# Small array tiles side by side in TensorE's order, a first join in four column groups, and a tap moved to ScalarE and GpSimd

## The chip, the cores and the metric

The kernel runs on one core of one Trainium2 chip. The metric is the device time of one launch in microseconds (us).

## The reference

The input is x, of shape (8, 1024, 128) in float32. A layer of gated linear attention with 8 heads of 128 comes first, then a mixture of 8 experts of which each token takes 2. The change touches the attention alone:

```python
q = _short_conv(x @ Wq, conv_q)                     # 8 heads; conv of 4 taps along time, then SiLU
k, v = _short_conv(x @ Wk, conv_k), _short_conv(x @ Wv, conv_v)   # 8 heads x 3 Householder steps each
beta, g = 2 * sigmoid(x @ Wb), -exp(A_log) * softplus(x @ Wa + dt_bias)
q, k = _l2norm(q) * d ** -0.5, _l2norm(k)
for t in time:                                      # S: one 128x128 state per head
    S = S * exp(g_t)
    for i in range(3):
        S = S + beta_i * outer(k_i, v_i - k_i @ S)
    o_t = q_t @ S
out = (rmsnorm(o) * silu(x @ Wg)) @ Wo              # then residual and layer norm
```

`_short_conv` adds four products: the input shifted by 0, 1, 2 and 3 tokens, each times a weight of its channel (a tap each), and takes SiLU of the sum.

## The kernel before

The 8192 tokens go through 64 superchunks of 128 tokens, of which each has four chunks (c = 0 to 3) of 32 tokens. A chunk has 32 x 3 = 96 rows of k and v, one for each Householder step. The recurrence over a chunk is written as a triangular system of 96x96 for each head, whose inverse is built in three diagonal blocks of 32 and joined from them.

Work is software-pipelined. In step (i, c) the engines project superchunk i (function `project`), prepare the chunk four before (gram products, `U`, `UQ`, `KD`), invert the diagonal blocks of the chunk five before, and run the chunk six before (join, solve, new state, read-out). Each step has 14 slots, k = 0 to 13, and in each slot one of the superchunk's 56 projection tiles (24 of v, 24 of k, 8 of q) is made. Four engines each follow a program of their own, in order, and meet at semaphores. The loop's body holds two superchunks.

TensorE. In slots 1, 3, 4, 6, 8, 10, 12, 13 (`INV_AT`) `invert` (L548, L550) issues an inversion step first: 24 products of 32x32 in array tiles of 32x32, eight heads by three blocks. Then comes the projection P of the slot (L530, full array, 128 channels by 131 tokens: three of them are the tokens before, for the taps). Then what the slot has: old_state in 1 and 4 (S against k and q, L562), rows_k in 1 and 3 (transposes of k, L572), the first join in 2 (16 products of 32 by 32 and 32 by 64 in PB), the second join in 4 (L660), the corner in 6 (L667), gram in 7 and 9 (L579), solve in 8 and 9 (L590), new_state in 10 and 11 (L605), read_out in 11 (L597), rows_v in 12 and 13. In c = 2 two groups of output transposes (slots 8, 10, L689) and the product with Wo (slot 12) are added, in c = 3 two gate products (slots 8, 10, L704) and the transpose of the next x. A projection waits until the taps of the tile two before have left its bank.

An inversion step k is one of eight: products 0 and 4 are copied to WB by ScalarE; the others are subtracted from Y by VectorE (L828, `inv_out`) into T or Y, and each next product waits for that. So INV_AT's slot 4 has the third step (index 2), slot 10 the sixth (index 5), slot 13 the eighth (index 7).

ScalarE. In each slot it copies the tile of the slot to CY times the first weight (tap 0, L736), does the slot's part (squares for norms L742 and L749, copies GA of the first join L753 and L754, YF L758 and L769, KD L764, BZ of the solved rows L774, VP), and applies SiLU (L808) to the tile of three slots before, which waits for its three other taps (semaphore taps_sb).

VectorE. In slot k it does taps 1, 2 and 3 of the tile of slot k - 1 (L819, a multiply and add from PSUM onto CY), and between them two groups of other work: the inversion's subtractions, the additions to the state S (L837), BZ (L885), U and UQ (L910, L912), the norm of the output (FA L893, OG L902).

GpSimd. In each step: the diagonal blocks of YF (L990), in c = 2 a power operation FB (L999), in c = 3 RS, then for each half of the heads S, KDS, E2, EM (L1004 to L1014), the power operation RT (L1017), the start Y1 of the inversion (L1024) and its masks UM (L1031).

CY has 7 buffers, PB is one PSUM bank that joins, output transposes, gate products, Wo and the transpose of x share.

Of the kernel before, what the change touches and what calls it, by code (L numbers as in the profile page):

```python
# [5 lines left out]
ALU = mybir.AluOpType  # L6
# [21 lines left out]
STEPS = 8  # L28
INV_AT = {1: 0, 3: 1, 4: 2, 6: 3, 8: 4, 10: 5, 12: 6, 13: 7}

# [84 lines left out]
def attention_part(nc, x, Wq, Wk, Wv, Wb, Wa, A_log, dt_bias, conv_q, conv_k, conv_v, Wg, rms_weight, Wo,  # L115
                   consts, x1):
    ctx = ExitStack()
    with ctx:
# [45 lines left out]
        with pctx:  # L164
# [211 lines left out]
        CY = sb("CY", [P, RING, P])  # L376
        SSR = sb("SSR", [P, CPS, NHEAD])
# [47 lines left out]
        corner = PB[:, 0:4 * BK].rearrange("p (g c) -> p g c", g=2)  # L425
        quad = PB[:, :].rearrange("p (h c) -> p h c", h=4)
# [10 lines left out]
            "xt_ps", "xt_sb", "proj_ps", "tap0_sb", "taps_sb", "kqv_sb"))  # L437
        kr_ps, ssr_sb, sse_sb, r2_sb, rt_sb, s1_sb, kds_sb, e2_sb, em_sb, kd_sb, kk_ps, u_sb = (
# [24 lines left out]
        def lagged(i, half, m):  # L463

            return (i - 1, 1 - half, m + TILES) if m < 0 else (i, half, m)

# [16 lines left out]
        with nc.Block() as block:  # L483
# [33 lines left out]
            def _(pe):  # L517
# [112 lines left out]
                def program(i, half, c):  # L630
# [7 lines left out]
                    for k in range(SLOTS):  # L638
                        if do_inv and k in INV_AT:
                            invert(invn, 1 - par, INV_AT[k])  # L640
                        if known(i, 0, NSC):
                            project(i, half, SLOTS * c + k)
# [4 lines left out]
                        if k == 2 and do_run:  # L647
                            pe.wait_ge(x3t_sb, run + 1)
                            side_bank_free(i, c, run, do_run)
                            mid, hi = slice(BK, 2 * BK), slice(2 * BK, R)  # L650
                            for h in range(NHEAD):
                                pe.matmul(join[mid, h, 0:BK], U[:, par, h, mid], X3[:, h, 0:BK], start=True, stop=True)
                                mm = pe.matmul(join[hi, h], U[:, par, h, hi], X3[:, h], start=True, stop=True)
                            mm.then_inc(join_ps, 1)
                        if k == 4 and do_run:
                            pe.wait_ge(join_sb, 3 * run + 1)
                            pe.sem_inc(begun, 1)
                            hi = slice(2 * BK, R)
                            for h in range(NHEAD):
                                mm = pe.matmul(join[BK:2 * BK, h, 0:BK], GA[hi, h, BK:2 * BK], Y3[hi, h], start=True, stop=True)  # L660
                            mm.then_inc(join_ps, 1)
                        if k == 6 and do_run:
                            pe.wait_ge(join_sb, 3 * run + 2)
                            pe.wait_ge(diag_sb, NBK * (run + 1))
                            for h in range(NHEAD):
                                j = h % LH
                                mm = pe.matmul(corner[CT * j:CT * j + CT, h // LH], GA[:, h, 0:BK], YF[:, h, BK:R], start=True, stop=True)  # L667
                            mm.then_inc(join_ps, 1)
# [4 lines left out]
                        if k == 11 and do_run:  # L673
                            read_out(run, rc)
# [16 lines left out]
                        if k in (8, 10) and gate_now:  # L691
                            l = (k - 8) // 2
# [13 lines left out]
                        if k == 12 and out_now:  # L706
                            pe.wait_ge(ogt_sb, 2 * (i - 1))
                            for h in range(NHEAD):
                                mm = pe.matmul(PB[:, 0:P], OGT[:, h], WO[:, h], start=(h == 0), stop=(h == NHEAD - 1))
                            mm.then_inc(wo_ps, 1)  # L710
                        if k == 12 and next_x:
                            if gate_now:
                                pe.wait_ge(gsil_sb, 2 * i)
                            transpose_x(i + 1, 1 - half)
# [6 lines left out]
            def _(act):  # L721
                def program(i, half, c):
# [4 lines left out]
                    for k in range(SLOTS):  # L727
# [3 lines left out]
                        if known(i, 0, NSC):  # L731
# [3 lines left out]
                            need(act, kqv_sb, T - RING + 1)  # L735
                            act.activation(CY[:, m % RING], ptile(m)[:, 0:P], ACT.Copy, scale=taps_of(m)[:, 0:1]).then_inc(tap0_sb, 1)  # L736
# [77 lines left out]
            def _(dve):  # L814
                def tap(j, m, s):
# [4 lines left out]
                                             ALU.mult, ALU.add).then_inc(taps_sb, 1)  # L820
# [119 lines left out]
                def program(i, half, c):  # L940
# [5 lines left out]
                    for k in range(SLOTS):  # L946
# [8 lines left out]
                        if taps:  # L955
                            tap(j, m, 3)
# [24 lines left out]
            def _(pool):  # L981
                def program(i, half, c):
# [9 lines left out]
                    if c == 3 and known(i - 2, 0, NSC):  # L992
                        pool.wait_ge(mv_sb, 2 * (i - 1))
                        need(pool, x1_sb, i - 2)
                        pool.tensor_tensor(RS[:, :], MV[:, 1:2], mhalf[:, 0:1], ALU.pow).then_inc(rs_sb, 1)
                    if c == 2 and known(i - 2, 0, NSC):
                        pool.wait_ge(fa_sb, 2 * (i - 1))
                        need(pool, og_sb, 2 * (i - 2))
                        pool.tensor_tensor(FB[:, :], FA[:, :], mhalf[:, :], ALU.pow).then_inc(fb_sb, 1)  # L999
                    if do_prep:  # L1000
# [461 lines left out]
```

## Time and profile before

| | |
|---|---|
| time, median of 3 runs | 8217.32 us (8217.16 to 8226.03) |
| profiled execution | 8217.97 us, its span 8215.9 |
| granted TensorE clock over the span | 0.944 of full speed |
| TensorE busy | 7423.3 us (90%) |
| VectorE busy | 6459.2 us (79%) |
| ScalarE busy | 5469.5 us (67%) |
| GpSimd busy | 4117.8 us (50%) |

The attention takes up to about 7165 us of the span, the experts the rest. PE is TensorE, DVE VectorE, ACT ScalarE, POOL GpSimd. Busy time counts instructions of arithmetic alone; matmuls are pipelined, so their modelled durations overlap, and the distance from start to start is the better measure of what one costs. In a timeline a row is one instruction, or several of one kind that follow each other (x48), and the square bracket at its end says how long the engine had sat idle before it and what it waited for.

### The profile page before, as it was taken

What the parts mean: (1) busy time and instruction counts of PE and PEld (TensorE: products, weight loads), DVE (VectorE), ACT (ScalarE), POOL (GpSimd) and SP (SyncE); (2) the same over time, 40 slices, a digit from 0 to 9 for tenths busy, and PEclk for the clock granted to TensorE, in tenths of its full rate; (3) what the DMA queues carried; (4) which work ended last, traced back from release to release, by engine and by line L of the source; (5) the groups of instructions that cost most, each with busy time, mean ns of one, the idle gap of its engine ahead of it and who ended that gap; (6) DMA issues with size and microseconds to landing.
All of it is one profiled execution on the core that took longest, in us unless ns stands there. A gap on an engine that the chain in (4) does not pass through costs nothing. (4 is left out here: it accounts for less than half of the span.)

```text
span 8215.9 us, 426591 instructions
## 1 busy us (share of the span) xinstructions
PE 7423.3 (90%) x155940; PEld 6296.7 (77%) x155940; DVE 6459.2 (79%) x22300; ACT 5469.5 (67%) x20343; POOL 4117.8 (50%) x6333
## 2 busy tenths in 40 slices
PE   5889999999999999999999899999989999889999
PEld 3777777777787777777777777777777777757777
DVE  4888888888888888888888888888888888623333
ACT  3777777777777777777777777777777777533333
POOL 0555555555555555555555555555555555511111
PEclk6899999999999999999999999999999999889999
DMA  2000000000000000000000000000000000010000
GB/s 90 8 10 9 10 9 10 9 10 9 10 10 9 10 10 10 9 10 9 10 9 10 9 10 9 10 9 10 10 9 10 9 10 10 7 32 8 10 8 8
DMA packets 283626, 97.69 MB, mean 12 GB/s; under 512 B 226097, under 2 KB 276545, under 8 KB 281153
## 3 DMA queue, kind: packets, MB, share of 16 engines
q1 hardware_dynamic: 281408, 68.93, 3.8%
q8 instruction: 1294, 21.20, 1.1%
q14 instruction: 924, 7.56, 0.3%
HBM read 52.08 MB, written 16.78 MB: 8 GB/s over the span
## 5 line engine op out<-in xcount | busy, mean ns | idle before, releaser
L819 DVE SCALAR_TENSOR_TENSOR CY<-PP,CWV,CY 128x128 f32<-128x128 f32 x4608 | 1585.5, 344 | 148.6 <-ACT CY L736 68.7
L819 DVE SCALAR_TENSOR_TENSOR CY<-PP,CWK,CY 128x128 f32<-128x128 f32 x4608 | 1581.4, 343 | 98.0 <-ACT CY L736 24.3
L1031 POOL TENSOR_TENSOR UM<-U,C 32x256 f32<-32x256 f32 x1536 | 1104.8, 719 | 120.2 <-POOL UM L1031 19.6
L1024 POOL TENSOR_TENSOR Y<-U,C 32x256 f32<-32x256 f32 x768 | 554.0, 721 | 1075.6 <-DVE UQ L912 1035.4
L550 PE MATMUL PI<-T,WB 32*32 32x32 f32 x49152 | 749.6, 196 | 303.2 <-DVE T L828 301.1
L550 PEld LDWEIGHTS PI<-T,WB 32*32 32x32 f32 x49152 | 639.0, 111 | 466.3 <-issue 403.2
L530 PE MATMUL PP<-XT,WV 128*128 128x131 f32 x3072 | 750.8, 328 | 188.5 <-issue 124.7
L530 PE MATMUL PP<-XT,WK 128*128 128x131 f32 x3072 | 783.6, 340 | 81.3 <-DVE CY L819 81.2
L736 ACT ACTIVATE CY<-PP,CWK 128x128 f32<-128x128 f32 x1536 | 564.4, 367 | 398.5 <-PE PP L530 387.4
L1004 POOL TENSOR_TENSOR S<-R,BETA 96x4 f32<-96x4 f32 x512 | 101.3, 198 | 1392.4 <-DVE R L872 1392.2
L736 ACT ACTIVATE CY<-PP,CWV 128x128 f32<-128x128 f32 x1536 | 567.2, 369 | 339.3 <-PE PP L530 328.0
L1237 ACT ACTIVATE HS<-PH,B1S 128x512 f32<-128x512 f32 x512 | 351.7, 687 | 607.8 <-PE PH L1156 607.7
L808 ACT ACTIVATE KQ<-CY 128x128 f32<-128x128 f32 x2048 | 741.7, 362 | 7.7
L1165 PEld LDWEIGHTS PY<-W2S,HS 128*128 128x128 f32 x4096 | 534.4, 192 | 218.2 <-issue 215.1
L530 PEld LDWEIGHTS PP<-XT,WV 128*128 128x128 f32 x3072 | 483.6, 198 | 267.2 <-issue 132.1
L742 ACT ACTIVATE EM<-PK 128x128 f32<-128x128 f32 x2048 | 536.2, 281 | 223.8 <-PE PK L572 223.5
L990 POOL TENSOR_TENSOR YF<-Y,ones 32x256 f32<-32x256 f32 x768 | 553.3, 720 | 250.8 <-issue 113.9
L837 DVE SCALAR_TENSOR_TENSOR S<-S,WHOLE,PK 128x128 f32<-128x128 f32 x2048 | 650.7, 339 | 14.0 <-PE PK L605 13.9
L885 DVE SCALAR_TENSOR_TENSOR BZ<-PA,HEADD,VP 128x128 f32<-128x128 f32 x2048 | 608.8, 338 | 64.3 <-PE PA L562 58.8
L530 PEld LDWEIGHTS PP<-XT,WK 128*128 128x128 f32 x3072 | 502.1, 206 | 159.1 <-DVE CY L819 102.8
L579 PE MATMUL PK<-KQ 128*96 128x128 f32 x4096 | 600.1, 294 | 13.1 <-ACT KD L764 2.1
L562 PE MATMUL PA<-S,KQ 128*128 128x128 f32 x4096 | 603.1, 295 | 1.2 <-DVE BZ L885 1.2
(228 smaller groups left out, 18910.8 us busy)
## 6 DMA issues: line engine op xcount, KB each, us to landing
EX<-exd SPq DMA_DIRECT2D x768, 32.0 KB
exd<-EXS SPq DMA_DIRECT2D x16, 512.0 KB, 2.6
XR<-in_L_attn_x SPq DMA_DIRECT2D x65, 64.0 KB, 3.1
XL<-in_L_attn_x SPq DMA_DIRECT2D x16, 256.0 KB, 2.8
XRES<-in_L_attn_x SPq DMA_DIRECT2D x64, 64.0 KB, 2.7
x<-X SPq DMA_DIRECT2D x64, 64.0 KB, 3.1
XI<-x SPq DMA_DIRECT2D x16, 256.0 KB, 2.9
out<-OUT SPq DMA_DIRECT2D x16, 256.0 KB, 2.3
```

The costliest lines, as they stand in the source:

```text
L530: pe.matmul(ptile(m), w, XT[:, half], start=True, stop=True).then_inc(proj_ps, 1)
L550: mm = pe.matmul(inv[r, h], WB[r, h], term[r, h], start=True, stop=True)
L562: mm = pe.matmul(PA[:, h % LH], KQ[:, rs, h, rc], S[:, h], start=True, stop=True)
L579: mm = pe.matmul(PK[0:R, h], kq[:, 0:R], kq, start=True, stop=True)
L736: act.activation(CY[:, m % RING], ptile(m)[:, 0:P], ACT.Copy, scale=taps_of(m)[:, 0:1]).then_inc(tap0_sb, 1)
L808: act.activation(to, CY[:, m % RING].rearrange("p (c t) -> p c t", c=CPS), ACT.Silu).then_inc(kqv_sb, 1)
L819: dve.scalar_tensor_tensor(CY[:, m % RING], ptile(m)[:, s:s + P], taps_of(m)[:, s:s + 1], CY[:, m % RING], ALU.mult, ALU.add).then_inc(tap ...
L837: op = dve.scalar_tensor_tensor(S[:, h], S[:, h], WHOLE[:, run, h:h + 1], PK[:, h], ALU.mult, ALU.add)
L885: op = dve.scalar_tensor_tensor(BZ[:, h], PA[:, h % LH], HEADD[:, run, h:h + 1], VP[:, par, h], ALU.mult, ALU.add)
L990: pool.tensor_tensor(YF[r, :, r], Y3[r, :, :], over(ones[r, 0:BK], [BK, NHEAD, BK], 1), ALU.mult).then_inc(diag_sb, 1)
L1024: pool.tensor_tensor(Y1[r, :, :], U[r, par, :, r], over(first[r, :], [BK, NHEAD, BK], 1), ALU.mult).then_inc(seed_sb, 1)
L1031: pool.tensor_tensor(UM[r, lv], U[r, par, :, r], over(merge[lv][r, :], [BK, NHEAD, BK], 1), ALU.mult).then_inc(made, 1)
```

## The change

The order of TensorE's instructions within slots changes. Inversion steps of slots 4, 10 and 13 (`INV_LAST`) are issued at the end of the slot, in slot 4 ahead of the second join, and in slot 10 ahead of read_out, which moves there from slot 11; in c = 3 the second gate product follows it. The corner of slot 6 and, in c = 3, the first gate product of slot 8 move ahead of the projection.

The first join writes its products to other partitions of PB: heads are spread over four column groups by their number's parity (`mids`, `his`), and ScalarE copies them with four instructions in place of two.

For the tiles of five slots, 0, 1, 5, 6 and 7 (`OFF`), ScalarE writes a second copy of the tile, shifted by three tokens and times the fourth weight, to CZ (4 buffers). VectorE does only taps 1 and 2 of these, and GpSimd adds CZ to CY (`last_tap`): tile 0 behind the diagonal blocks, tile 1 behind FB, tiles 5, 6, 7 behind RT. SiLU of such a tile waits for the new semaphore tap3_sb.

```diff
+OFF = (0, 1, 5, 6, 7)
+NOFF = len(OFF) * CPS
 INV_AT = {1: 0, 3: 1, 4: 2, 6: 3, 8: 4, 10: 5, 12: 6, 13: 7}
+INV_LAST = (4, 10, 13)
+INV_FIRST = [k for k in INV_AT if k not in INV_LAST]
...
+        mids = PB[:, 0:4 * BK].rearrange("p (q c) -> p q c", q=4)
+        his = PB[:, 0:8 * BK].rearrange("p (q c) -> p q c", q=4)
...
@@ TensorE, for k in range(SLOTS)
-                        if do_inv and k in INV_AT:
+                        if do_inv and k in INV_FIRST:
                             invert(invn, 1 - par, INV_AT[k])
+                        if k == 6 and do_run:
+                            ...                                  # the corner, as it was
+                        if k == 8 and gate_now:
+                            ...                                  # the gate product l = 0, as it was
                         if known(i, 0, NSC):
                             project(i, half, SLOTS * c + k)
...
                             for h in range(NHEAD):
-                                pe.matmul(join[mid, h, 0:BK], U[:, par, h, mid], X3[:, h, 0:BK], start=True, stop=True)
-                                mm = pe.matmul(join[hi, h], U[:, par, h, hi], X3[:, h], start=True, stop=True)
+                                q, o = h // 2, 1 - h % 2
+                                pe.matmul(mids[CT * o:CT * o + CT, q], U[:, par, h, mid], X3[:, h, 0:BK], start=True, stop=True)
+                                o = 2 + h % 2
+                                mm = pe.matmul(his[CT * o:CT * o + CT, q], U[:, par, h, hi], X3[:, h], start=True, stop=True)
...
-                        if k == 11 and do_run:
-                            read_out(run, rc)
...
+                        if do_inv and k in INV_LAST:
+                            invert(invn, 1 - par, INV_AT[k])
+                        if k == 4 and do_run:
+                            ...                                  # the second join, as it was
+                        if k == 10 and do_run:
+                            read_out(run, rc)
+                        if k == 10 and gate_now:
+                            ...                                  # the gate product l = 1, as it was
...
@@ ScalarE
+                            if k in OFF:
+                                act.activation(CZ[:, off_rank(m) % ZRING], ptile(m)[:, 3:3 + P], ACT.Copy, scale=taps_of(m)[:, 3:4])
                             act.activation(CY[:, m % RING], ptile(m)[:, 0:P], ACT.Copy, scale=taps_of(m)[:, 0:1]).then_inc(tap0_sb, 1)
...
-                            act.activation(GA[BK:2 * BK, :, 0:BK], join[BK:2 * BK, :, 0:BK], ACT.Copy, scale=-1.0)
-                            act.activation(GA[2 * BK:R], join[2 * BK:R], ACT.Copy, scale=-1.0).then_inc(join_sb, 1)
+                            for e in range(2):
+                                o = CT * (1 - e)
+                                act.activation(GA[BK:2 * BK, e:NHEAD:2, 0:BK], mids[o:o + CT], ACT.Copy, scale=-1.0)
+                                o = CT * (2 + e)
+                                op = act.activation(GA[2 * BK:R, e:NHEAD:2], his[o:o + CT], ACT.Copy, scale=-1.0)
+                            op.then_inc(join_sb, 1)
...
-                            act.wait_ge(taps_sb, 3 * (T + 1))
+                            if m % SLOTS in OFF:
+                                act.wait_ge(tap3_sb, NOFF * j + off_rank(m) + 1)
+                            else:
+                                act.wait_ge(taps_sb, 3 * (T + 1))
...
@@ VectorE
-                                             ALU.mult, ALU.add).then_inc(taps_sb, 1)
+                                             ALU.mult, ALU.add).then_inc(taps_sb, 2 if s == 2 and m % SLOTS in OFF else 1)
...
-                        if taps:
+                        if taps and m % SLOTS not in OFF:
                             tap(j, m, 3)
...
@@ GpSimd
+                def last_tap(i, m):
+                    pool.wait_ge(taps_sb, 3 * (TILES * i + m + 1))
+                    pool.tensor_tensor(CY[:, m % RING], CY[:, m % RING], CZ[:, off_rank(m) % ZRING], ALU.add).then_inc(tap3_sb, 1)
```

## Rows read from the trace of the kernel before

**Rows 1.** The page's first part: busy time and share of each engine.
```profile
PE 7423.3 (90%) x155940; PEld 6296.7 (77%) x155940; DVE 6459.2 (79%) x22300; ACT 5469.5 (67%) x20343; POOL 4117.8 (50%) x6333
```

**Rows 2.** Waits of TensorE, 600 to 6900 us: total us, times, longest.
```profile
PE PI L550 <- DVE T L828: 275.1, 203, 2.3
```

**Rows 3.** Timeline of VectorE, subtraction T2: start us, us, instruction.
```profile
3014.35 0.41 DVE L828 TENSOR_TENSOR T<-Y,PI 96x256 f32<-96x256 f32 x1
...
3040.66 0.41 DVE L828 TENSOR_TENSOR T<-Y,PI 96x256 f32<-96x256 f32 x1
...
3064.53 0.41 DVE L828 TENSOR_TENSOR T<-Y,PI 96x256 f32<-96x256 f32 x1
...
3092.52 0.41 DVE L828 TENSOR_TENSOR T<-Y,PI 96x256 f32<-96x256 f32 x1
...
3120.23 0.41 DVE L828 TENSOR_TENSOR T<-Y,PI 96x256 f32<-96x256 f32 x1
...
3175.78 0.41 DVE L828 TENSOR_TENSOR T<-Y,PI 96x256 f32<-96x256 f32 x1
...
3205.11 0.41 DVE L828 TENSOR_TENSOR T<-Y,PI 96x256 f32<-96x256 f32 x1
```

**Rows 4.** Timeline of TensorE, the projection of slot 7 in each chunk.
```profile
3034.26 0.49 PE L530 MATMUL PP<-XT,WV 128*128 128x131 f32 x2
...
3058.12 0.49 PE L530 MATMUL PP<-XT,WV 128*128 128x131 f32 x2
...
3084.88 0.81 PE L530 MATMUL PP<-XT,WK 128*128 128x131 f32 x2
...
3112.88 0.49 PE L530 MATMUL PP<-XT,WQ 128*128 128x131 f32 x2 [0.25 <-DVE CY L819]
```

**Rows 5.** Timeline of TensorE, the third inversion product of c = 2.
```profile
3078.74 0.70 PE L550 MATMUL PI<-T,WB 32*32 32x32 f32 x48 [2.28 <-DVE T L828]
```

**Rows 6.** Windows: stretch, us, busy PE, PEld, DVE, ACT, POOL, clock, DMA, GB/s.
```profile
3078.60:3087.30 8.70, 8.56 (x152) 7.30 (x152) 7.26 (x27) 6.65 (x29) 6.17 (x11) 0.61 0.09 16
```

**Rows 7.** Timeline of TensorE in c = 1, slots 7 to 11.
```profile
3058.71 1.11 PE L579 MATMUL PK<-KQ 128*96 128x128 f32 x8
...
3062.76 1.04 PE L590 MATMUL PK<-BZ,YF 96*96 96x128 f32 x8
3063.73 0.70 PE L550 MATMUL PI<-Y,WB 32*32 32x32 f32 x48
3064.36 0.49 PE L530 MATMUL PP<-XT,WK 128*128 128x131 f32 x2
3064.69 1.05 PE L605 MATMUL PK<-BZ,KD 96*128 96x128 f32 x8
...
3066.48 1.16 PE L605 MATMUL PK<-BZ,KD 96*128 96x128 f32 x8
3067.57 0.70 PE L550 MATMUL PI<-T,WB 32*32 32x32 f32 x48
```

**Rows 8.** Timeline of ScalarE in c = 1, the copy of the solved rows.
```profile
3063.84 0.59 ACT L774 ACTIVATE BZ<-PK 96x512 f32<-96x512 f32 x1 [0.41 <-PE PK L590]
```

**Rows 9.** Timeline of VectorE: fourth inversion's subtraction, two taps, start of the output's norm.
```profile
3044.45 0.42 DVE L828 TENSOR_TENSOR T<-Y,PI 96x256 f32<-96x256 f32 x1 [0.41 <-PE PI L550]
...
3057.61 0.72 DVE L819 SCALAR_TENSOR_TENSOR CY<-PP,CWV,CY 128x128 f32<-128x128 f32 x2
...
3076.44 0.17 DVE L893 TENSOR_SCALAR FA<-QSE 128x8 f32<-128x8 f32 x1 [0.78 <-ACT OGT L749]
```

**Rows 10.** Groups of instructions: busy us, mean ns of one | idle before, releaser.
```profile
L736 ACT ACTIVATE CY<-PP,CWV 128x128 f32<-128x128 f32 x1536 | 567.2, 369 | 339.3 <-PE PP L530 328.0
...
L754 ACT ACTIVATE GA<-PB 32x512 f32<-32x512 f32 x256 | 150.5, 588 | 3.0
...
L1017 POOL TENSOR_TENSOR RT<-SSE,half 128x8 f32<-128x8 f32 x256 | 421.8, 1648 | 0.0
...
L1014 POOL TENSOR_TENSOR EM<-E,C 96x128 f32<-96x128 f32 x512 | 237.2, 463 | 0.0
```

More of the change, by code:

```diff
@@ L638, in program @@
                     for k in range(SLOTS):
-                        if do_inv and k in INV_AT:
+                        if do_inv and k in INV_FIRST:
                             invert(invn, 1 - par, INV_AT[k])
+                        if k == 6 and do_run:
+                            pe.wait_ge(join_sb, 3 * run + 2)
+                            pe.wait_ge(diag_sb, NBK * (run + 1))
+                            for h in range(NHEAD):
+                                j = h % LH
+                                mm = pe.matmul(corner[CT * j:CT * j + CT, h // LH], GA[:, h, 0:BK], YF[:, h, BK:R], start=True, stop=True)
+                            mm.then_inc(join_ps, 1)
+                        if k == 8 and gate_now:
+                            l = 0
+                            if l == 0:
+                                if do_run:
+                                    pe.wait_ge(join_sb, 3 * run + 3)
+                                if known(i - 2, 0, NSC):
+                                    pe.wait_ge(y_sb, i - 1)
+                            else:
+                                pe.wait_ge(gsil_sb, 2 * (i - 1) + 1)
+                            wg = WG[:, :].rearrange("p (g j d) -> p g j d", g=2, j=LH)
+                            for cc in range(2):
+                                t0 = HALO + CT * (2 * l + cc)
+                                for j in range(LH):
+                                    mm = pe.matmul(quad[CT * j:CT * j + CT, 2 * cc:2 * cc + 2], XT[:, 1 - half, t0:t0 + CT], wg[:, :, j], start=True, stop=True)
+                            mm.then_inc(gate_ps, 1)
                         if known(i, 0, NSC):
@@ L690, in program @@
                             mm.then_inc(ogt_ps, 1)
-                        if k in (8, 10) and gate_now:
-                            l = (k - 8) // 2
+                        if k == 12 and out_now:
+                            pe.wait_ge(ogt_sb, 2 * (i - 1))
+                            for h in range(NHEAD):
+                                mm = pe.matmul(PB[:, 0:P], OGT[:, h], WO[:, h], start=(h == 0), stop=(h == NHEAD - 1))
+                            mm.then_inc(wo_ps, 1)
+                        if k == 12 and next_x:
+                            if gate_now:
+                                pe.wait_ge(gsil_sb, 2 * i)
+                            transpose_x(i + 1, 1 - half)
+                        if do_inv and k in INV_LAST:
+                            invert(invn, 1 - par, INV_AT[k])
+                        if k == 4 and do_run:
+                            pe.wait_ge(join_sb, 3 * run + 1)
+                            pe.sem_inc(begun, 1)
+                            hi = slice(2 * BK, R)
+                            for h in range(NHEAD):
+                                mm = pe.matmul(join[BK:2 * BK, h, 0:BK], GA[hi, h, BK:2 * BK], Y3[hi, h], start=True, stop=True)
+                            mm.then_inc(join_ps, 1)
+                        if k == 10 and do_run:
+                            read_out(run, rc)
+                        if k == 10 and gate_now:
+                            l = 1
                             if l == 0:
@@ L705, in program @@
                             mm.then_inc(gate_ps, 1)
[L706 to L714, printed above, removed]
                 pe.wait_ge(ready, READY)
@@ L999, in program @@
                         pool.tensor_tensor(FB[:, :], FA[:, :], mhalf[:, :], ALU.pow).then_inc(fb_sb, 1)
+                    if known(i, 0, NSC):
+                        for k in OFF:
+                            if k in (1, 2):
+                                last_tap(i, SLOTS * c + k)
                     if do_prep:
```

30 lines of the change are left out of this document (16 added, 14 removed).

## The prediction

> **What bounds the kernel now.** I read the page's busy times first [rows 1]: TensorE is busy for 90% of the span, VectorE for 79%, ScalarE for 67%, GpSimd for 50%. None is full, so busy shares don't say which wait ends last. The table of waits for TensorE comes next [rows 2]: its largest entry in the main loop is 275 us at the inversion products, each of which needs a subtraction made by VectorE. The two engines hand work to each other in a ring. I split it at two points of each chunk and read their times in the timelines of both engines. The points are T2, the subtraction that follows the sixth inversion product (slot 10) [rows 3], and P7, TensorE's projection of slot 7 [rows 4].
>
> From T2 to P7 of the next chunk (the VectorE leg) VectorE works without a gap through its slots 10 to 13 and 0 to 5, and TensorE waits. From P7 to T2 (the TensorE leg) TensorE's products stand one behind the other, and VectorE waits. The four chunks of the superchunk shown:
> c0: 3014.35 to 3034.26 = 19.91, to 3040.66 = 6.40, sum 26.31.
> c1: to 3058.12 = 17.46, to 3064.53 = 6.41, sum 23.87.
> c2: to 3084.88 = 20.35, to 3092.52 = 7.64, sum 27.99.
> c3: to 3112.88 = 20.36, to 3120.23 = 7.35, sum 27.71.
> In all 105.88 us. The next superchunk, the other half of the loop's body, has 29.33 for c2 (3175.78 to 3205.11) in place of 27.99. There are 64 superchunks, so 1 us in each is 64 us in the whole.
>
> c2 holds a clock effect. Before the third inversion product TensorE sits idle for 2.28 us [rows 5], and in the stretch that follows the granted clock is 0.61, a mixture of the full level (2.4 GHz) and the half one (1.2 GHz), while it is busy for 8.56 of 8.70 us [rows 6].
>
> **The order of TensorE's products.** Three inversion products (slots 4, 10, 13) go behind the other work of their slot, so that they meet other products in small array tiles; the corner join (slot 6) goes ahead of its projection, and read_out from slot 11 to 10. From start to start, the 24 tile products of an inversion step before a full-size one take 0.63 (3063.73 to 3064.36), and a projection 0.33 behind tile products (to 3064.69). Behind the corner join P7 takes 0.59 until the gram products (3058.12 to 3058.71) [rows 4, 7]; without a change of tile form I put it at 0.22, a third below the 0.33, an estimate, so 0.37 goes there. Counted blindly, the three meetings in a chunk and the shorter join save 1.3 us of TensorE per chunk.
>
> In the TensorE leg, however, T2 hangs on the sixth inversion product, and this is the one that goes back. Before, it starts right behind the second solve (0.97, 3062.76 to 3063.73) and covers the wait for ScalarE's copy of the solved rows, which starts at 3063.84, that is 1.08 after the solve's start, and takes 0.59 [rows 8]. After, the order is solve, projection 10, new_state 0, inversion. new_state 0 can't start before the copy is there: 1.08 + 0.59 + about 0.06 to hand over = 1.73 behind the solve's start; the projection covers only a part, some 0.4 us is idle. A new_state takes 1.09 to the inversion product behind it (3066.48 to 3067.57), and from the start of an inversion product to its subtraction it is 0.80 (3063.73 to 3064.53). I use 0.75 of it, since the subtraction here is already awaited, and VectorE has no tap in front. The second solve starts 4.64 after P7 (3062.76 − 3058.12); less the 0.37, plus 0.08 because a transposition of VectorE and the corner's merge stand nearer to it, 4.35. The new leg is 4.35 + 1.73 + 1.09 + 0.75 = 7.92, where 6.41 was: +1.5 in c0 and c1. With no idle time it would be 7.5; with a projection in front at full price 8.1. In c2 and c3 the same steps give 7.64 + 1.76 = 9.4 and 7.35 + 1.55 = 8.9, since output transpositions and gate products stand beside them (bounds ±0.3).
>
> **The fourth tap.** For 5 of 14 tiles VectorE does two taps, not three. A tap is 0.36 (0.72 for two) [rows 9]; started behind one another they come every 0.26 to 0.37. So VectorE loses 5 × 0.33 = 1.65 of work per chunk. But tiles 0 and 1 alone lie in the VectorE leg: 2 × 0.37 = 0.75. The taps of tiles 5, 6, 7 stand where VectorE waits for TensorE, and I count them at 0 (bounds 0 and 1.0). Of the waits in that leg, the one for the fourth inversion product, 0.41 at 3044.45 [rows 9], goes for the most part: −0.36. Against this, the third inversion product stands behind old_state 1: +0.17. ScalarE gets five more copies, 0.37 each [rows 10], 5 × 0.25 to 5 × 0.37 = 1.3 to 1.9 a chunk, hidden by its idle third except in slots 0 to 3. GpSimd gets five additions of 128x128; the nearest operation, 96x128, is 0.46 [rows 10]; bounds 0.40 and 0.73. 5 × 0.46 = 2.3 us on an engine that is idle half the time: free.
>
> A page bears on this. The Trainium skill, "SBUF — State Buffer", section "SBUF: two separate sides", says that an operation of GpSimd and one of VectorE with two SBUF inputs exclude each other for the whole instruction. The taps read PSUM and SBUF, so only the eight gated products of the output in each superchunk (L902) qualify. If every one waited for an addition of 0.46 with the chance of its share of time, about 8%, the rule would make 512 × 0.46 × 0.08 = 19 us, and the sum below 19 higher; no row here shows such a wait.
>
> **The first join.** In four column groups its 16 products overlap; I expect 0.45 less of TensorE (bounds 0 and 0.7). ScalarE's copies become four instead of two: the large one is 0.59 for 512 columns [rows 10], and two of 256 columns lie between that and half of it, so the four are 0.3 to 0.6 longer; I take 0.34. These copies stand ahead of the SiLU on which rows_k 1 waits.
>
> **VectorE leg, chunk by chunk.** c1: 17.46 − 0.75 − 0.36 + 0.17 − 0.1 = 16.4. c0: there TensorE waits for ScalarE's SiLU behind the four copies (+0.34) and has the third inversion behind projection 4 and old_state 1 (+0.6), which takes back the 0.75: 20.0. c2: VectorE waits 0.78 for ScalarE's squares at 3076.44 [rows 9], which come earlier by the two taps and by some 0.3 of waits behind them (−1.05, an estimate); that brings the idle time before the third inversion below the present 2.28, and if the clock stays full the 8.70 us of [rows 6] give back 8.7 × 0.39 × 0.6 = 2.0, of which I take 1.9 (0.39 is what the clock lacks, 0.6 my share of the stretch in which TensorE is what the others wait for): 17.4. c3: −0.75 and −0.36 as in c1, the 0.25 that P7 waits for a tap at 3112.88 [rows 4], and 0.45 of such waits before it, an estimate: 18.55.
>
> **Sum.** c0 20.0 + 7.92 = 27.9 (+1.6); c1 16.4 + 7.92 = 24.3 (+0.45); c2 17.4 + 9.4 = 26.8 (−1.2); c3 18.55 + 8.9 = 27.45 (−0.25). In the other half of the body c2 has 1.34 more to give back; I credit half, over all superchunks a quarter of 1.34: −0.3. Together +0.3 (+1.6 + 0.45 − 1.2 − 0.25 − 0.3), and since each of these is rounded I take +0.3 to +0.4: 64 × 0.39 = +25 us. The profiled execution took 8217.97 and its span 8215.9; the median is 8217.3. 8218 + 25 = 8243.
>
> **Rivals.**
> A, faster: the waits shrink with the work. Ring or no ring, TensorE and VectorE each lose 1.3 to 1.65 us a chunk; if the waits keep their size, 256 × 1.3 = 333 us go: 7885. Half of it gives 8050. For it: taps and joins stand in the dense stretches of c0 to c3 too. Against it: the sixth inversion product is moved behind the wait for ScalarE.
> B, slower: the clock. If the third inversion product, later by P4 and old_state 1, makes the idle time before it longer in c2, or if the new 0.4 us idle before new_state 0 is enough, the half level comes in more chunks. One such stretch costs the same 2.0 us. One more in each superchunk is 64 × 2.0 = +128 on top of the sum, 8370. It decides once the idle time is over the 2.28 of rows 5; idle times of about 1 us elsewhere are not followed by it.
> C, slower: the SiLU waits for GpSimd's addition behind the power operations of GpSimd, 1.65 us each [rows 10], of which 0.7 would show in one chunk: +45, 8285.
>
> **How the numbers follow.** The forecast 0.46, with its own range 8170 to 8300, of which 0.12 is faster, 0.15 the same, 0.19 slower. A 0.26. B 0.20. C 0.08. A measurement of this kernel tells 0.2%, 16 us, from no change. Faster 0.12 + 0.26 = 0.38; same 0.15; slower 0.19 + 0.28 = 0.47. The range for 8 in 10 is 8060 to 8390: it leaves out half of A, and little of B.
>
> **What would show it.** (1) In the TensorE leg of c1 the sixth inversion product starts behind new_state 0, T2 is 7.9 behind P7, and new_state 0 shows an idle time of 0.4 to 0.5 before it, ended by ScalarE's copy. (2) The VectorE leg of c1 is 16.4. (3) The third inversion product of c2 has less than 2 us of idle time before it and the clock in the stretch behind it is near 1. (4) GpSimd's additions take 0.40 to 0.73, ScalarE's busy time grows by 256 × 1.9 = 490 us or less, VectorE's falls by 256 × 5 × 0.34 = 440. The forecast is wrong if c0's legs don't grow, if T2 is no later than 7.0 behind P7, or if c2 keeps its half clock.

## The result, and the profile after

The changed kernel takes 8617.9 us (median of 4 runs, 8613.0 to 8624.9) against 8221.7: the ratio is 1.0488 (95% interval 1.0463 to 1.0513). It is slower by 4.9%, where 8243 was forecast and 8390 was the end of the range. The profiled execution took 8624.9, its span 8623.1, 407 us more than before.

The first part of the page of the changed kernel, in the form of [rows 1]:

```profile
PE 7426.9 (86%) x155940; PEld 6321.4 (73%) x155940; DVE 6039.5 (70%) x21020; ACT 5803.5 (67%) x22135; POOL 4670.7 (54%) x7613
```

Work moved as forecast: VectorE 420 us less, GpSimd 553 more, ScalarE 334 more. TensorE is busy as long as before, but that equality is the sum of two opposite changes: in the attention's part its busy time at the half level of the clock grew from 656 to 956 us, and at the full level it shrank from 5529 to 5220. By the sum the 407 us are idle time, so the waits come first. TensorE's waits in the main loop (us in total, times, longest), to hold against [rows 2]:

```profile
PE PP L544 <- DVE CY L861: 484.1, 557, 4.9
PE PK L619 <- ACT BZ L813: 119.9, 219, 0.5
PE PI L562 <- DVE Y L870: 87.6, 192, 0.6
```

and those of VectorE in the same stretch:

```profile
DVE T L870 <- PE PI L564: 554.5, 384, 3.2
DVE CY L861 <- ACT CY L771: 300.1, 474, 2.4
```

Before, TensorE waited 275 us for VectorE's subtractions. That entry is gone. In its place VectorE waits 555 us for the inversion products (138 before), and projections wait 484 us for taps (132 before). VectorE works in order: a tap behind a subtraction that waits is late too, and a projection that needs the tap's bank waits with it.

The two legs of the prediction, as means over chunks 12 to 239, from the starts of T2 and P7 in both traces (before, after, in us; c0 holds the return of the loop in every second superchunk):

| | VectorE leg | forecast change | TensorE leg | forecast change |
|---|---|---|---|---|
| c0 | 22.42, 23.82: +1.40 | +0.1 | 6.41, 8.43: +2.02 | +1.5 |
| c1 | 17.54, 16.52: −1.02 | −1.06 | 6.36, 8.70: +2.34 | +1.5 |
| c2 | 20.65, 18.21: −2.44 | −2.95 | 7.91, 10.61: +2.70 | +1.76 |
| c3 | 20.23, 19.15: −1.08 | −1.8 | 7.31, 9.81: +2.50 | +1.55 |

Together +6.42 in a superchunk, times 64 = 411 us.

A timeline of TensorE after, c = 1, slots 5 to 11 (the P7 of this chunk is at 3215.51):

```profile
3213.14 0.49 PE L544 MATMUL PP<-XT,WV 128*128 128x131 f32 x2 [0.62 <-DVE CY L861]
...
3215.51 0.49 PE L544 MATMUL PP<-XT,WV 128*128 128x131 f32 x2 [0.44 <-DVE CY L861]
...
3220.18 1.04 PE L604 MATMUL PK<-BZ,YF 96*96 96x128 f32 x8
3221.05 0.39 PE L544 MATMUL PP<-XT,WK 128*128 128x131 f32 x2
3221.99 1.13 PE L619 MATMUL PK<-BZ,KD 96*128 96x128 f32 x8 [0.55 <-ACT BZ L813]
3223.05 0.70 PE L564 MATMUL PI<-Y,WB 32*32 32x32 f32 x48
```

and of VectorE, the taps that wait for ScalarE and the subtraction T2:

```profile
3218.29 0.81 DVE L861 SCALAR_TENSOR_TENSOR CY<-PP,CWV,CY 128x128 f32<-128x128 f32 x2 [0.37 <-ACT CY L771]
3220.03 0.35 DVE L861 SCALAR_TENSOR_TENSOR CY<-PP,CWV,CY 128x128 f32<-128x128 f32 x1 [0.93 <-ACT CY L771]
...
3223.81 0.42 DVE L870 TENSOR_TENSOR T<-Y,PI 96x256 f32<-96x256 f32 x1 [1.77 <-PE PI L564]
```

The reader is to see three things. TensorE is idle for 0.55 before new_state 0, until ScalarE has copied the solved rows. The inversion product starts 1.06 behind that, and VectorE sits idle for 1.77 until it is done. And projections 5 and 7 wait for taps, 0.62 and 0.44, where before none of the two did. In other chunks it is more: projection 7 waits 1.09 in c0, 0.9 in c2 and 1.21 in c3 as means, and in c3 projection 53 (slot 11) waits 1.35 in every superchunk, where it was 0.27 before:

```profile
3282.40 0.49 PE L544 MATMUL PP<-XT,WQ 128*128 128x131 f32 x2 [1.35 <-DVE CY L861]
```

The granted clock over the span fell from 0.944 to 0.926: the stretches at the half level add up to 672 us before and 993 after. Those that begin in c2 shrank from 459 to 238, as forecast; those of c0, c1 and c3 together grew from 211 to 751. At the full level the 300 us more of busy time would take half; so the clock's part in the loss is some 150 us at most, an estimate. No run has the changed kernel with its clock kept.

The prices of the single operations: ScalarE and GpSimd, groups of instructions after (busy us, mean ns), beside [rows 10]:

```profile
L770 ACT ACTIVATE CZ<-PP,CWV 128x128 f32<-128x128 f32 x640 | 236.7, 370 | 189.0 <-PE PP L544 181.1
...
L792 ACT ACTIVATE GA<-PB 32x256 f32<-32x256 f32 x512 | 192.2, 375 | 5.9
...
L790 ACT ACTIVATE GA<-PB 32x128 f32<-32x128 f32 x512 | 136.7, 267 | 17.8 <-PE PB L691 8.6
...
L1026 POOL TENSOR_TENSOR CY<-CY,CZ 128x128 f32<-128x128 f32 x1280 | 570.7, 455 | 739.1 <-DVE CY L861 738.6
```

The second copy takes 370 ns, GpSimd's addition 455 (forecast 460), and GpSimd is early: it waits 739 us for VectorE, and no wait of ScalarE's SiLU for it stands in the table of waits (rival C did not come).

### The profile page after: what moved, and what is told of

It is laid out like the page before. It is cut to its first block and busy times, and to the rows that moved or that the text cites. A ratio compares the mean times of both kernels' runs of the same rounds, so it can differ in the third digit from the quotient of the medians.

```text
span 8623.1 us, 429552 instructions
## 1 busy us (share of the span) xinstructions
PE 7426.9 (86%) x155940; PEld 6321.4 (73%) x155940; DVE 6039.5 (70%) x21020; ACT 5803.5 (67%) x22135; POOL 4670.7 (54%) x7613
## 5 line engine op out<-in xcount | busy, mean ns | idle before, releaser
L861 DVE SCALAR_TENSOR_TENSOR CY<-PP,CWV,CY 128x128 f32<-128x128 f32 x3968 | 1365.9, 344 | 286.5 <-ACT CY L771 224.9
L861 DVE SCALAR_TENSOR_TENSOR CY<-PP,CWK,CY 128x128 f32<-128x128 f32 x4096 | 1406.5, 343 | 93.3 <-ACT CY L771 33.9
L1026 POOL TENSOR_TENSOR CY<-CY,CZ 128x128 f32<-128x128 f32 x1280 | 570.7, 455 | 739.1 <-DVE CY L861 738.6
L544 PE MATMUL PP<-XT,WK 128*128 128x131 f32 x3072 | 745.3, 326 | 196.3 <-DVE CY L861 195.2
L870 DVE TENSOR_TENSOR T<-Y,PI 96x256 f32<-96x256 f32 x1024 | 421.9, 412 | 668.9 <-PE PI L564 668.2
L544 PEld LDWEIGHTS PP<-XT,WV 128*128 128x128 f32 x3072 | 504.0, 207 | 427.0 <-DVE CY L861 283.1
L564 PE MATMUL PI<-T,WB 32*32 32x32 f32 x49152 | 729.3, 193 | 6.4 <-issue 4.0
L564 PEld LDWEIGHTS PI<-T,WB 32*32 32x32 f32 x49152 | 613.5, 108 | 153.5 <-issue 63.3
L619 PE MATMUL PK<-BZ,KD 96*128 96x128 f32 x4096 | 563.6, 281 | 141.3 <-ACT BZ L813 141.3
L576 PE MATMUL PA<-S,KQ 128*128 128x128 f32 x4096 | 652.5, 311 | 12.5 <-DVE BZ L927 2.3
```

Of the source, the lines that this page charges most:

```text
L544: pe.matmul(ptile(m), w, XT[:, half], start=True, stop=True).then_inc(proj_ps, 1)
L564: mm = pe.matmul(inv[r, h], WB[r, h], term[r, h], start=True, stop=True)
L576: mm = pe.matmul(PA[:, h % LH], KQ[:, rs, h, rc], S[:, h], start=True, stop=True)
L619: mm = pe.matmul(PK[:, h], KD[:, rc, h], BZ[0:R, h], start=True, stop=True)
L861: dve.scalar_tensor_tensor(CY[:, m % RING], ptile(m)[:, s:s + P], taps_of(m)[:, s:s + 1], CY[:, m % RING], ALU.mult, ALU.add).then_inc(tap ...
L1026: pool.tensor_tensor(CY[:, m % RING], CY[:, m % RING], CZ[:, off_rank(m) % ZRING], ALU.add).then_inc(tap3_sb, 1)
```

## The experiments

Each time is a median, each ratio is to the kernel before on the same chip, with its 95% interval. The kernel before took 8206 to 8230 us on these chips, so a difference between two experiments in us is known to some 20 us.

**The three parts alone.** Each is the kernel before with one part of the change.

`e_taps`: the diff's parts of OFF, CZ, last_tap and tap3_sb alone.

> The kernel before with the fourth-tap part alone (five tiles' last product on ScalarE and GpSimd). Theory (the order of TensorE's products makes the loss: VectorE waits, in order, for inversion products that come later, taps queue behind that wait and projections behind the taps): this part is a gain, the VectorE leg shorter by 0.75 to 1.1 us a chunk, 8000 to 8150 us. Rival (the way over ScalarE and GpSimd makes the loss: SiLU late, ScalarE's queue longer): 8350 to 8600.

Measured: 8246.6 us, ratio 1.0047 (1.0031 to 1.0064). Neither: a small loss, where the theory wanted a gain. The leg of VectorE in c1 is shorter by 0.90 (17.54 to 16.64), as forecast, but the TensorE leg is longer by 0.75 (6.36 to 7.11). The waits point at it. TensorE's in this kernel:

```profile
PE PP L544 <- DVE CY L855: 141.7, 318, 4.6
PE PP L544 <- issue: 116.9, 28, 4.5
PE PK L593 <- ACT KD L797: 88.0, 235, 0.7
```

and VectorE's:

```profile
DVE CY L855 <- ACT CY L769: 422.9, 720, 1.0
DVE T L864 <- PE PI L564: 158.8, 312, 0.8
```

The gram products, which waited for nothing here before, wait 88 us for KD, since ScalarE's copies of tiles 5 to 7 stand ahead of KD's in its queue. And VectorE waits 423 us for tap 0 (87 before): CZ is written ahead of CY. The other order wasn't tried.

`e_join`: the four column groups and the four copies alone.

> The kernel before with the first join in four column groups alone. Theory: its products cost 0.4 us less of TensorE, ScalarE's four copies 0.3 more; 8180 to 8260 us. Rival (the longer copies delay the SiLU and the second join): 8300 to 8400.

Measured: 8700.2 us, ratio 1.0587 (1.0553 to 1.0620), the largest loss of all, from the part that costs TensorE less. Both theories missed. The timeline of TensorE, c = 1, slots 3 to 5:

```profile
3250.92 0.60 PE L586 MATMUL PK<-C,KQ 128*128 128x128 f32 x4
3253.10 0.70 PE L564 MATMUL PI<-T,WB 32*32 32x32 f32 x48 [1.58 <-DVE T L870]
3253.73 0.78 PE L544 MATMUL PP<-XT,WV 128*128 128x131 f32 x2
3254.31 1.91 PE L576 MATMUL PA<-S,KQ 128*128 128x128 f32 x8
3256.15 1.06 PE L731 MATMUL PB<-Y,GA 32*32 32x32 f32 x16
```

and the window over it (us, then busy time of PE, PEld, DVE, ACT, POOL, then the clock):

```profile
3251.50:3261.50 10.00, 8.42 (x149) 7.39 (x149) 7.73 (x28) 6.91 (x29) 5.68 (x11) 0.61 0.03 6
```

The third inversion product starts when VectorE has made its subtraction, no earlier. A join that ends sooner only makes the idle time before it longer: 1.58 here, where the same wait was about 1.1 before. Counted over 600 to 6900 us of each trace, a wait being followed by the half clock when a stretch of it begins less than 6 us later, it was 1 of 57 such waits in c1 before and is 21 of 53 now; in the one shown old_state 1 takes 1.91, not 1.05. In this trace the half level adds up to 1857 us, against 672.

`e_order`: the order of TensorE's products alone.

> The kernel before with the new order of TensorE's products alone, all three taps on VectorE and the old first join. Theory: the whole loss and a little more, as VectorE has no relief: 8600 to 8800 us, VectorE's idle time before its T subtractions over 500 us in all. Rival (the taps or the join make the loss): 8200 to 8300.

Measured: 8578.5 us, ratio 1.0450 (1.0419 to 1.0480). The order alone makes nearly the whole loss: the changed kernel is at 1.0488. VectorE is idle for 519 us before its T subtractions (the theory: over 500), and TensorE's projections wait 542 us for taps; the time is 21 us below the theory's range. The parts don't add up: 0.5, 5.9 and 4.5% make 4.9%. Behind the new order the third inversion product no longer follows idle time (no such row stands in TensorE's waits), so the join can't do there what it does alone. It still shows in c0 of the changed kernel: rows_k 1 waits 1.32 as a mean for ScalarE's SiLU, 0.65 with the order alone, 0.58 before.

**One inversion product at a time.**

`e_i5front`, from the changed kernel:

```diff
-INV_LAST = (4, 10, 13)
+INV_LAST = (4, 13)
```

> The changed kernel with the sixth inversion product (slot 10) back in front of its slot, read_out still in slot 10. Theory of the prediction (this one move lengthens the TensorE leg by 1.5 us a chunk, measured 2.0 to 2.7): 8617 less 256 x 1.5 to 2.3, so 8030 to 8230 us. Rival (all three moves lose alike, the third and eighth product too, and the clock): 8400 to 8500.

Measured: 8314.0 us, ratio 1.0125 (1.0096 to 1.0154): 304 us of the 396 come back by this one product, more than the rival allows and less than the theory wanted.

`e_i5only`, from the kernel before: the product of slot 10 alone behind its slot's work.

> The kernel before with the sixth inversion product alone (slot 10) moved behind the slot's projection and new_state 0. Theory (TensorE leg: 0.45 idle before new_state 0, 1.1 for it, and VectorE's wait in front of its additions and taps): the leg from P7 to T2 grows by 1.5 to 2 us in each chunk, the time by 256 x 1.1 to 1.5, 8500 to 8600 us. Rival (the three moves lose together): about 8340.

Measured: 8654.3 us, ratio 1.0510 (1.0488 to 1.0533): 425 us, more than the end of the theory's range. The TensorE leg grows as it says but for c2 (c0 to c3: +1.90, +1.86, +2.41, +1.89; 1.5 to 2 was expected), and the VectorE leg of c0 by 1.9 too. The timeline of TensorE in c = 3, slots 9 to 11, shows what the prediction had left out:

```profile
3203.76 0.39 PE L544 MATMUL PP<-XT,WQ 128*128 128x131 f32 x2
3204.70 1.13 PE L619 MATMUL PK<-BZ,KD 96*128 96x128 f32 x8 [0.55 <-ACT BZ L807]
3205.76 0.70 PE L564 MATMUL PI<-Y,WB 32*32 32x32 f32 x48
3206.39 1.07 PE L744 MATMUL PB<-WG,XT 128*32 128x256 f32 x16
3209.24 0.54 PE L544 MATMUL PP<-XT,WQ 128*128 128x131 f32 x2 [1.78 <-DVE CY L855]
...
3210.73 2.08 PE L619 MATMUL PK<-BZ,KD 96*128 96x128 f32 x8
```

and VectorE beside it:

```profile
3206.52 0.42 DVE L864 TENSOR_TENSOR T<-Y,PI 96x256 f32<-96x256 f32 x1 [1.77 <-PE PI L564]
3206.86 0.34 DVE L855 SCALAR_TENSOR_TENSOR CY<-PP,CWQ,CY 128x128 f32<-128x128 f32 x1
3207.23 1.58 DVE L912 TENSOR_SCALAR QSE<-SSR 32x8 f32<-32x8 f32 x4
3208.84 0.74 DVE L855 SCALAR_TENSOR_TENSOR CY<-PP,CWQ,CY 128x128 f32<-128x128 f32 x2
```

The window behind it:

```profile
3209.20:3218.00 8.80, 8.52 (x147) 7.06 (x150) 4.99 (x18) 3.55 (x13) 2.72 (x5) 0.61 0.01 3
```

VectorE waits 1.77 for the late product. Behind that in its queue stand a tap, the four sums QSE (1.58) and the third tap. Tile 53 (slot 11 of c3) is one of the two tiles whose projection waits for taps one tile nearer (CLOSE), and it needs that third tap: TensorE is idle for 1.78, and then runs at clock 0.61. Stretches at half clock that begin in slot 11 of c3 appear 38 times in this trace and add up to 341 us; before there is none.

`e_i5_close`, the same with the near tile put elsewhere:

```diff
-PBANK, CLOSE = [0, 1], (19, 53)
+PBANK, CLOSE = [0, 1], (19, 50)
```

> The sixth inversion product alone moved behind its slot's work (8654 us, 425 more than before), and the second tile whose projection waits for the taps one tile nearer (CLOSE) put at tile 50 (slot 8 of c = 3) in place of 53 (slot 11). Theory: in c = 3 projection 53 waits for taps that stand in VectorE's queue behind the late sixth subtraction (1.8 us of idle time of TensorE), and 341 us of half clock follow; without this the time falls by 1.8 to 3 us a superchunk, 8460 to 8560 us, and the half-clock stretches that begin in slot 11 of c = 3 go. Rival (the longer chain from P7 to T2 is all of it, and the wait only overlaps it): 8620 to 8680.

Measured: 8523.2 us, ratio 1.0356 (1.0336 to 1.0377): 131 us less, as the theory says, and no stretch at half clock begins in slot 11 of c3. The VectorE leg of c0 falls from 24.28 to 21.73. The half level falls from 1065 to 536 us. So at least some 130 of the 425 us are the queue behind the wait and its clock. The other 300 (1.16 us a chunk) are what is left: the longer chain, less what the VectorE legs give back, and the near tile in its new place, which isn't free either, since projection 50 waits 1.01 for taps in every superchunk and the TensorE leg of c3 is 1.04 longer for it.

`e_i2only` and `e_i7only`: the products of slot 4 or of slot 13 alone.

> The kernel before with the third inversion product alone (slot 4) moved behind projection and old_state 1. Theory (projections no longer stand behind TensorE's wait for VectorE, but VectorE's wait and its taps get later): the wait is filled, the half clock of c = 2 goes, 8130 to 8230 us; the loss of the new order is then at slots 10 and 13. Rival (each of the three moves costs a third of the 370 us): 8300 to 8370.

Measured: 8242.8 us, ratio 1.0001 (0.9968 to 1.0034). Neither range holds it: no change beyond the interval, where the theory wanted up to 90 us less. The half clock of c2 did go for the most part (459 to 150 us), but in c0, c1 and c3 it grew from 211 to about 450. A wait of TensorE for subtractions turned into one for taps: projections wait 458 us (132 before).

> The kernel before with the eighth inversion product alone (slot 13) moved behind the slot's projection and rows_v 1. Theory (VectorE's subtraction in slot 13 waits for it, and its taps of tile 12 stand behind; TensorE saves one change of tile form): +0.2 to +0.5 us a chunk, 8260 to 8350 us. Rival (hidden): 8217, or 8190 by the saved change.

Measured: 8291.2 us, ratio 1.0068 (1.0045 to 1.0091), in the theory's range. VectorE waits for the eighth product, in this kernel 222 us in total (103 before):

```profile
DVE Y L864 <- PE PI L564: 222.0, 172, 2.5
```

`e_lateout`, the changed kernel with VectorE's subtractions of slots 4 and 10 behind the third tap:

```diff
-                    if do_inv and k in INV_AT and INV_AT[k] not in (0, 4) and part == 0:
+                    if do_inv and k in INV_AT and INV_AT[k] not in (0, 4) and part == 0 and k not in LATE_OUT:
...
+                        if do_inv and k in LATE_OUT:
+                            inv_out(invn, INV_AT[k])
```

> The changed kernel with VectorE's subtractions of slots 4 and 10 moved behind the third tap of their slot, so that the taps no longer queue behind the wait for TensorE. Theory (in-order taps behind VectorE's wait, and projections behind these taps, make a part of the loss beside the longer chain): PE's wait for taps falls from 484 us to under 300, the time to 8350 to 8500. Rival (the chain of inversion products alone is what ends last): 8600 to 8700, as each subtraction is later.

Measured: 8472.1 us, ratio 1.0302 (1.0271 to 1.0333), 146 us less than the changed kernel, although the two subtractions stand later in VectorE's queue. TensorE's wait for taps, 484 us in the changed kernel, is here:

```profile
PE PP L545 <- DVE CY L862: 305.3, 489, 4.8
```

The theory's range holds the time; its count for the wait (under 300) is missed by 5 us. The gain sits in one leg: the VectorE leg of c0 falls from 23.82 to 21.04 (the seven others together are 0.7 longer), and projection 53, which waited 1.35 in every superchunk of the changed kernel, doesn't wait here.

**The clock by itself.** `e_join_keep` and `e_keep` put extra products of 256 columns ahead of the third inversion product, in PI's free quadrant; they compute nothing that is used.

```diff
+                        if do_inv and k == 4:
+                            for _ in range((0, 2, 4, 2)[c]):      # e_keep: (0, 0, 4, 0)
+                                pe.matmul(PI[R:P, 2 * P:4 * P], ident[:, 0:CT], C[:, 0:2 * P], start=True, stop=True)
```

> The kernel with the first join in four column groups alone (8700 us), with two (c = 1, 3) or four (c = 2) extra products of 256 columns in slot 4, written to a free quadrant of PSUM, ahead of the third inversion product, where TensorE otherwise is idle. Theory (the shorter join lengthens the idle time before the third inversion product, and the half clock that follows makes the loss): half-clock time falls from 1857 us to under 900, and the time to 8150 to 8300, though TensorE has more to do. Rival (ScalarE's four copies and what waits for them make the loss): 8700 to 8900.

Measured: 8129.6 us, ratio 0.9908 (0.9876 to 0.9940), 571 us less than without them, and the half level falls from 1857 to 304 us. The clock was most of the join's loss; the theory's range was even short by 20. Not all of it: beside `e_keep`, which has the old join and the same four products in c2, this kernel is still 60 us slower.

> The kernel before with four such extra products in slot 4 of c = 2 alone, where 2.28 us of idle time stand before the third inversion product and the granted clock falls to 0.61. Theory: the half-clock stretches of c = 2 (459 us in all) mostly vanish, 8050 to 8180 us. Rival (the clock is not a matter of that idle time): 8217 to 8300.

Measured: 8069.2 us, ratio 0.9832 (0.9803 to 0.9862). No stretch at half clock begins in c2 any more (459 us before), 205 us are left in all. The timeline of TensorE around the third inversion product, c = 2, beside [rows 5] (an extra product is two instructions; the first row shows the last six of eight):

```profile
3015.81 1.46 PE L655 MATMUL PI<-C 128*32 128x256 f32 x6
3018.07 0.70 PE L564 MATMUL PI<-T,WB 32*32 32x32 f32 x48 [0.80 <-DVE T L867]
...
3019.03 1.05 PE L576 MATMUL PA<-S,KQ 128*128 128x128 f32 x8
```

Old_state takes 1.05 behind it, the full level's price.

**Fewer tiles, and the sums.** `e_taps01`: as `e_taps`, with

```diff
-OFF = (0, 1, 5, 6, 7)
+OFF = (0, 1)
```

> The kernel before with the fourth tap of tiles 0 and 1 alone on ScalarE and GpSimd. Theory (the tiles of slots 5 to 7 bring ScalarE's copies ahead of KD, for which the gram products wait, 88 us, and lengthen the TensorE leg by 0.75; those of slots 0 and 1 shorten the VectorE leg by 0.9): 8000 to 8120 us. Rival (ScalarE's second copy stands ahead of tap 0 in any slot, and VectorE waits for it, 423 us): 8200 to 8260.

Measured: 8128.7 us, ratio 0.9903 (0.9876 to 0.9929), 118 us less than with five tiles. The VectorE leg of c1 is 16.70, the TensorE leg 6.31: the gain stays, the loss is gone. TensorE's wait for KD is gone from the table. VectorE's wait for tap 0 is 135 us, so the rival was right for the tiles of slots 5 to 7 at most. The time is 9 us outside the theory's range.

`e_keep_taps01`: the two gains together.

> The kernel before with both gains: the fourth tap of tiles 0 and 1 on ScalarE and GpSimd, and four extra products before the third inversion product of c = 2. Theory (one shortens the VectorE leg, the other keeps the clock; they add): 7970 to 8030 us. Rival (the shorter leg removes the idle time that the extra products fill, so these delay TensorE): 8070 to 8130.

Measured: 7939.1 us, ratio 0.9645 (0.9625 to 0.9665), the best of all. The two gains were 1.0 and 1.7%; together they give 3.55%, more than the sum, and 31 us below the theory's range. This version beats both kernels. The first part of its page:

```profile
PE 7341.5 (92%) x156452; PEld 6166.5 (78%) x156452; DVE 6287.0 (79%) x21788; ACT 5530.9 (70%) x20855; POOL 4342.9 (55%) x6845
```

`e_best_join`: this, with the four column groups of the first join, and (0, 1, 4, 1) extra products.

> The old order of products, the fourth tap of tiles 0 and 1 off VectorE, the first join in four column groups, and extra products ahead of the third inversion product (none, 1, 4, 1 in c = 0 to 3). Theory (with the clock kept, the shorter join gives 0.2 to 0.4 us a chunk): 7850 to 7940 us. Rival (ScalarE's four copies delay the SiLU that rows_k waits for in c = 0, as 8130 against 8069 showed): 7960 to 8060.

Measured: 8066.2 us, ratio 0.9801 (0.9765 to 0.9837), 127 us worse, by two edits at once. The rival's place is right (its range ends 6 us earlier): the transposes of rows_k wait 77 us for ScalarE's SiLU (40 without the join), and in c0 137 us at half clock follow such a wait of about 1.5.

`e_repaired`: the changed kernel with `INV_LAST = (4, 13)` and `OFF = (0, 1)`.

> The changed kernel with two of its parts taken back: the sixth inversion product in front of its slot again, and the fourth tap off VectorE for tiles 0 and 1 alone. Theory (sum of parts: 8314 with the product in front, less about 100 for the taps of slots 5 to 7, as between 8247 and 8129): 8190 to 8250 us. Rival (the leg with these taps is hidden by the other moves): 8290 to 8330.

Measured: 8347.0 us, ratio 1.0142 (1.0118 to 1.0167). The theory missed, the rival's place is right (its range ends 17 us earlier): taking three tiles' taps off ScalarE gives 118 us in the old order, and nothing in this one (1.0125 with five tiles). Projections wait 412 us for taps there, so relief of VectorE in slots 5 to 7 is worth as much as ScalarE's longer queue costs. That reason was only argued, no run tells the two apart.

## Why the prediction was wrong

The direction was right, the size was not: +25 us forecast, about +400 measured. In a superchunk +6.4 us stand against +0.3: the TensorE legs miss by 3.25, the VectorE legs by 2.6, and the 0.3 credited for the other half of the body didn't show. (The terms as they stand make +0.3, 19 us; 25 were taken.) By its steps:

1. The chain of the sixth inversion product was right in its links. In the chunk shown after: new_state 0 starts 1.81 behind the second solve (forecast 1.73), the inversion product 1.06 behind that (1.09), T2 0.76 later (0.75). The means of c0, c1 and c3 are the same three numbers. The first link was mis-sized: from P7 to the second solve it takes 4.67, not 4.35, in this chunk, and as a mean it grew by 0.16, 0.48, 0.55 and 0.65 in c0 to c3 where 0.29 less was forecast. That is 3.0 of the 3.25 us by which the TensorE legs miss (9.6 us a superchunk against 6.3), about 190 of 210 us. The saved change of tile form exists: with the order alone c0 has 4.31, where 4.64 was. But with the order alone the link is longer by 0.53 in c1 and 0.63 in c2, and with the taps alone by 0.90, 0.75 and 0.51 in c0 to c2. In the changed kernel the fifth inversion product (slot 8) waits for VectorE's Y (88 us, 13 before), and in the chunk shown the second gram product starts 0.52 behind its projection, 0.23 before.
2. The step that failed is the one that counted a later T2 as a longer TensorE leg and no more. A wait was added on VectorE (1.77 before T2 in every chunk but c2, where it is 2.23; none before), and what is queued behind it wasn't named: taps, and behind them projections, above all the near tiles 19 (the 0.62 before projection 5 in c1) and 53 (1.35 in the changed kernel, 1.78 in `e_i5only`). `e_lateout` (146 us) and `e_i5_close` (131 us) show it for tile 53, whose wait lies in the VectorE leg of c0. The VectorE legs of c0, c2 and c3 gave 1.3, 0.5 and 0.7 less than forecast, some 160 us of the miss; that those of c2 and c3 come from the same waits is argued, no run takes them away alone.
3. c1's VectorE leg was right (16.52 for 16.4), and so was c2's clock (238 us for 459). But the idle times of about 1 us that "are not followed by it" were made a rule from one superchunk. It held for the kernel before (1 of 115 idle times of 0.8 to 1.4 us was followed by the half level, counted as in `e_join`), not for the changed one: there it is 97 of 310, for the most part in slot 7 of c0, c2 and c3, at projection 53 and in slot 4 of c2. So rival B, the clock elsewhere, came true at c0, c1 and c3, 540 us more at the half level, without the idle time over 2.28 that it asked for. (The wait of 0.41 that was taken off the VectorE leg did go, but it belongs to the seventh inversion product, slot 12, not to the fourth.)
4. The fourth tap was taken as free on ScalarE except in slots 0 to 3. The copies in slots 5 to 7 are the ones that cost: 118 us between `e_taps` and `e_taps01`.
5. The first join costs TensorE 0.4 less as forecast (from its first product to the inversion product behind it 0.59, 1.02 before), and ScalarE's four copies take 1.28 together where two took 0.96 (+0.32, forecast 0.34). In c0 the copies cost more than their length: rows_k 1 waits 1.32 where 0.58 was. Alone, this gain in front of a wait is the largest loss.
6. Of the rule of the Trainium skill ("SBUF — State Buffer", section "SBUF: two separate sides"): VectorE's eight gated products (OG) grew, as its group of instructions after shows.

```profile
L944 DVE SCALAR_TENSOR_TENSOR OG<-OSB,FB,GSIL 128x128 f32<-128x128 f32 x512 | 205.3, 439 | 1.8 <-POOL FB L1049 1.8
```

Before, the same 512 take 163.0 us, 358 ns each. What GpSimd does at the start of each tells them apart. With GpSimd idle they take 342 before (260 of them) and 339 after (70); those that start beside one of its products EM take 480 as a mean before (81, up to 660), and those beside an addition of CZ take 438 after (124, up to 548). With the order alone, without any addition on GpSimd, it is:

```profile
L938 DVE SCALAR_TENSOR_TENSOR OG<-OSB,FB,GSIL 128x128 f32<-128x128 f32 x512 | 184.0, 399 | 1.8 <-POOL FB L1043 1.8
```

So operations of VectorE with two SBUF inputs do get longer beside GpSimd's products and additions, by up to 420 ns, no more than the length of one of these (888 and 463 for the two kinds of EM, 455 for the addition). That agrees with the rule. Its "whole instruction" doesn't hold for all: beside the power operation RT of 1.65 us, 161 of the gated products take 324 ns before, no longer than alone. Half of the 42 us comes with the order, as other work of GpSimd now lies beside them. It is a tenth of the loss at most.

## What to carry to other kernels

When an instruction is moved back in one engine's order, list what stands behind the wait for it in the other engine's queue, and who waits for each of these; of the 425 us that one moved product cost here, at least 130 were the queue behind one such wait and the clock that followed. A gain of TensorE that ends in front of a wait is idle time, and may be worse than none: look at the granted clock of the stretch behind the wait, in every stage, before such a gain is booked. And where idle time can't be removed, four useless products in it gained 1.7%.

## What the runs showed of the hardware

TensorE's clock was the largest single lever of the study: in the kernel with the new join, eight more products a superchunk took 571 us off (8700 to 8130). Idle times of TensorE that the half level followed, counted as in `e_join`: 1 of 115 of 0.8 to 1.4 us in the kernel before, 72 of 133 of 1.4 to 1.75 in `e_join`, 54 of 58 of 2.28 before. But the idle time isn't all: of 310 of 0.8 to 1.4 us in the changed kernel 97 were followed by it, and 5 of 128 in `e_keep`. What sets these apart no run shows. Four extra products in the wait of c2 were enough to keep the full level there (`e_keep`).
